# A four-layer convolution and expert-mixing kernel: two differences of the first pair move to GpSimd, and VectorE shares all evictions of the matrix sets from the third to the fourteenth

## The reference

```python
x = x + conv1d(x, w_L0, kernel=9, pad=4, groups=4) + (cond @ cw_L0.T + bias)[:, :, None]
x = x + einsum('boi,bih->boh', sum_k att1[b, k] * W_L1[k], x) + (att1 @ bias_k1)[:, :, None]
x = x + conv1d(x, w_L2, kernel=9, pad=4, groups=4) + (cond @ cw_L2.T + bias)[:, :, None]
x = x + einsum('boi,bih->boh', sum_k att3[b, k] * W_L3[k], x) + (att3 @ bias_k3)[:, :, None]
```

## Time and profile before

| | us |
|---|---|
| median of three runs | 2477.7 |
| lowest, highest | 2477.03, 2478.44 |
| span of the profiled execution, first to last instruction | 2475.0 |
| TensorE busy in the profiled execution | 2456.7 (99%) |
| VectorE busy | 2139.8 (86%) |
| ScalarE busy | 1520.3 (61%) |
| GpSimd busy | 23.4 (1%) |

### The profile page before, as it was taken

The page is one execution under the profiler, slowest core; times in us unless marked ns, Lnnn a source line. Parts: engine busy times, 40 slices in busy tenths (PEclk is TensorE's granted clock), DMA queues, the critical chain, the costliest instruction groups (busy, mean ns, idle before and its releaser), DMA issues.

```text
span 2475.0 us, 99123 instructions
## 1 busy us (share of the span) xinstructions
PE 2456.7 (99%) x45256; PEld 1482.8 (60%) x45256; DVE 2139.8 (86%) x806; ACT 1520.3 (61%) x1120; POOL 23.4 (1%) x28
## 2 busy tenths in 40 slices
PE   8999999999999999999999999999999999999998
PEld 4444444555555555566666666666666666666665
DVE  7988988988988889889889888898898898888984
ACT  6666666666666666666666666666666666665665
POOL 3000000000000000000000000000000000000000
PEclk9999999999999999999999999999999999999999
DMA  9644444444445444444444444444444444444433
GB/s 346 207 131 127 152 144 127 135 152 136 127 138 156 130 127 155 142 127 138 152 135 127 140 155 128 127 157 140 127 140 151 133 127 143 153 127 127 157 108 121
DMA packets 186683, 357.24 MB, mean 144 GB/s; under 512 B 12754, under 2 KB 143834, under 8 KB 154010
## 3 DMA queue, kind: packets, MB, share of 16 engines
q1 hardware_dynamic: 186056, 354.60, 45.7%
q10 hardware_dynamic: 594, 2.13, 0.3%
HBM read 205.69 MB, written 150.99 MB: 144 GB/s over the span
## 4 chain that ended last, share of the span: by engine, by line
PE 97%; DVE 2%; issue 1%; ACT 0%; DVEq 0%; ACTq 0%
PE psum L410 61%; PE psum L481 35%; DVE diff L754 1%; PE psum L379 0%; ACT shared L629 0%; PE psum L353 0%; PE psum L331 0%; ACT diff L629 0%; DVE y L797 0%; DVE y L813 0%; DVE y L838 0%; DVE h L789 0%; ACT y L629 0%; DVE y L816 0%; DVE outb L861 0%
## 5 line engine op out<-in xcount | busy, mean ns | idle before, releaser
L410 PE MATMUL psum<-diff,prod_w 32*64 32x512 f32 x28672 | 1689.2, 588 | 2.9 <-DVE diff L754 0.9
L410 PEld LDWEIGHTS psum<-diff,prod_w 32*64 32x64 f32 x28672 | 963.0, 131 | 624.3 <-issue 295.2
L754 DVE TENSOR_TENSOR diff<-xin 128x2052 f32<-128x2052 f32 x256 | 993.0, 3934 | 286.7 <-PE psum L410 286.7
L481 PE MATMUL psum<-y,mixw 32*64 32x512 f32 x16384 | 1028.9, 588 | 1.9 <-DVE y L816 1.9
L481 PEld LDWEIGHTS psum<-y,mixw 32*64 32x64 f32 x16384 | 581.5, 132 | 338.2 <-issue 179.5
L754 DVE TENSOR_TENSOR diff<-x 128x2055 f32<-128x2055 f32 x255 | 570.4, 2320 | 0.0
L720 ACT ACTIVATE x<-psum,bias_now 128x2048 f32<-128x2048 f32 x128 | 251.7, 1966 | 198.7 <-PE psum L481 198.7
L680 ACT ACTIVATE outb<-psum,bias_now 128x2048 f32<-128x2048 f32 x128 | 251.1, 1962 | 195.3 <-PE psum L481 195.3
L645 ACT COPY shared<-psum 128x2048 f32<-128x2048 f32 x128 | 238.9, 1866 | 171.6 <-PE psum L410 171.6
L838 DVE TENSOR_TENSOR y<-y,shared 128x2048 f32<-128x2048 f32 x126 | 291.2, 2311 | 14.7 <-ACT y L659 14.7
L673 ACT COPY y<-psum 128x2048 f32<-128x2048 f32 x126 | 235.7, 1871 | 91.8 <-PE psum L410 91.8
(11 more groups left out here) (80 smaller groups left out, 106.7 us busy)
## 6 DMA issues: line engine op xcount, KB each, us to landing
xin<-x SPq DMA_DIRECT2D x128, 1024.0 KB, 6.9
out<-outb SPq DMA_DIRECT2D x127, 1024.0 KB, 4.8
mixw<-mix_dram SPq DMA_DIRECT2D x512, 128.0 KB, 5.5
mix_dram<-shared SPq DMA_DIRECT2D x6, 1024.0 KB, 12.7
mix_dram<-y SPq DMA_DIRECT2D x6, 1024.0 KB, 10.4
mix_dram<-diff SPq DMA_DIRECT2D x2, 1024.0 KB, 12.1
mix_dram<-outb SPq DMA_DIRECT2D x2, 1024.0 KB, 14.1
y<-experts ACTq DMA_DIRECT2D x2, 512.0 KB, 4.3
```

The costliest lines, as they stand in the source:

```text
L410: return pe.matmul(psum[cols, half, g, :], prod_w[v][at, kind, s, cols], moving, start=start, stop=stop, skip_group_check=True)
L481: mm = pe.matmul(psum[cols, half, r, :], mixw[home][at, b, g, cols], y[home][at, :, g, b, :], start=g == 0, stop=g == GROUPS - 1)
L754: nc.vector.tensor_tensor(into(kind), in0, in1, op).then_inc(diff_ready[v], 1)
```

## The change

1. GpSimd makes BOTH and SIGNED of pair 0 (`first_diff`), each counted on a new semaphore `first_diffs`. BOTH comes ahead of layer one's tap weights and waits for x of the first pair; SIGNED comes behind them. VectorE makes ONLY_EVEN and ONLY_ODD of pair 0 alone, and each adds two to `diff_ready[0]`, so that later counts stay.
2. `HALVED` now holds 2 to 13. VectorE takes two banks of each of those twelve sets, all ahead of its differences, and waits for the same landed stores as ScalarE from set 10 on.
3. TensorE's first convolution waits for VectorE's halves of sets 12 and 13 too, and for `first_diffs`; its third part waits for `diff_ready[0]` at 4 as before. SyncE waits for `first_diffs` too ahead of x of pair 1.

```diff
-        HALVED = (2, 3, 4, 5, 6)
+        HALVED = tuple(range(2, AHEAD))
...
             load_mix_on(sp, 0, 0)
+            sp.wait_ge(first_diffs, 2)
             sp.wait_ge(diff_ready[0], PRODUCTS)
...
+            def first_diff(kind, op):
+                eighths = xin[:].rearrange("p (m c) -> p c m", c=BLOCK)
+                pool.tensor_tensor(diff_of(0, kind).rearrange("p (s c) -> p s c", s=PH)[:, :, 0:T - 1],
+                                   eighths[:, 0:PH, 1:T], eighths[:, PH:, 0:T - 1], op).then_inc(first_diffs, 1)
+
             for v in range(2):
...
+                if v == 0:
+                    pool.wait_ge(x_loaded, 16 * PB)
+                    pool.wait_ge(edges_clear, 1)
+                    first_diff(BOTH, ALU.add)
                 pool.wait_ge(taps_loaded[v], 16 * 3)
...
                 pool.tensor_tensor(w[:, SIGNED], middle, w[:, SIGNED], ALU.subtract).then_inc(taps_ready, 1)
+                if v == 0:
+                    first_diff(SIGNED, ALU.subtract)
...
-                pe.wait_ge(diff_ready[v], diffs[0])
+                pe.wait_ge(diff_ready[v] if made is None else made, diffs[0])
...
-                pe.wait_ge(diff_ready[v], diffs[1])
+                pe.wait_ge(diff_ready[v] if made is None else made, diffs[1])
                 pe.wait_ge(sem_b, count_b)
+                if made is not None:
+                    pe.wait_ge(*upper_taken(AHEAD - 1))
...
-                    conv(0, 0, taken(AHEAD - 2), taken(AHEAD - 1), (1, 2, 4), nothing)
+                    pe.wait_ge(*upper_taken(AHEAD - 2))
+                    conv(0, 0, taken(AHEAD - 2), taken(AHEAD - 1), (1, 2, PRODUCTS), nothing, made=first_diffs)
...
             for j in HALVED:
                 dve.wait_ge(agg_pe, j + 1)
+                if j >= 10:
+                    dve.wait_ge(agg_stored[same_home_before(j)], 16)
                 nc.vector.tensor_copy(homes[home_of[j]][:, PH // 2:PH], psum[:, half_of(j), PH // 2:PH, :]
                                       ).then_inc(agg_taken["dve"], 1)
             dve.wait_ge(edges_clear, 1)
-            diff_of_xin(0, (BOTH, SIGNED, ONLY_EVEN, ONLY_ODD))
+            diff_of_xin(0, (ONLY_EVEN, ONLY_ODD))
```

More of the change, by code:

```diff
@@ L133, in conditioned_layers @@
         x_loaded = sem("x_loaded")
+        first_diffs = sem("first_diffs")
         diff_ready = [sem(f"diff_ready{v}") for v in range(2)]
@@ L424, in divided_set, with conv @@
                 return mm
-            def conv(v, n, a_free, b_free, diffs, late, halves=(A, B_HALF), second=nothing, odd=None):
+            def conv(v, n, a_free, b_free, diffs, late, halves=(A, B_HALF), second=nothing, odd=None, made=None):
                 A, B_HALF = halves
@@ L737, in diff_of_xin @@
                 at = [eighths[:, PH * (q % 2):PH * (q % 2 + 1), q // 2:q // 2 + T - 1] for q in range(4)]
-                make_diffs(0, at, kinds, lambda kind: diff_of(0, kind).rearrange(
+                make_diffs(0, n, at, kinds, lambda kind: diff_of(0, kind).rearrange(
                     "p (s c) -> p s c", s=PH)[:, :, 0:T - 1])
@@ L747, in diff_of_x2, with make_diffs @@
                 at = [x2[:, start:start + size] for start in (HALF - 1, 0, HALF, 1)]
-                make_diffs(1, at, kinds, lambda kind: diff_of(1, kind)[:, 0:size])
-            def make_diffs(v, at, kinds, into):
+                make_diffs(1, n, at, kinds, lambda kind: diff_of(1, kind)[:, 0:size])
+            def make_diffs(v, n, at, kinds, into):
                 for kind in kinds:
@@ L753, in make_diffs @@
                                     SIGNED: (at[2], at[1], ALU.subtract), ONLY_ODD: (at[3], at[1], ALU.subtract)}[kind]
-                    nc.vector.tensor_tensor(into(kind), in0, in1, op).then_inc(diff_ready[v], 1)
+                    nc.vector.tensor_tensor(into(kind), in0, in1, op).then_inc(diff_ready[v], PRODUCTS // len(kinds)
+                                                                               if whole(n) and (v, n) == (0, 0) else 1)
             nc.vector.memset(hid[0]["att_t"][:], 0.0).then_inc(blank, 1)
```

## The result

The changed kernel takes 2482.82 us (median of 13 runs, 2481.99 to 2484.23) against 2477.59 us before (13 runs, 2476.84 to 2479.47): 5.2 us slower, a ratio of 1.0021 with a 95% interval of 1.0013 to 1.0028. The profiled execution of the changed kernel has a span of 2482.1 us and took 2483.88 us. So 1.8 us lie around that span, and 1.8 to 1.9 in every run on record, not 2.7.

A forecast was written before the change was run, and what follows sets the result against it. TensorE holds 96% of the chain, and the start of the first convolution's third part sets the end. Its 6.75 us delay plus 0.25 for the clock made 7.0, so 2484.7 us; range 2478.8 to 2487.5, forecast's own 2482.6 to 2485.9.

The forecast's parts named there:

- What bounds: Start of the kernel: any shift of the first convolution's third part moves VectorE's first output and the end equally.
- T3: Start of the first convolution's third part, which needs ONLY_EVEN: 43.9 before, forecast 50.65, 6.75 us later.
- the restart: TensorE going on after waiting for VectorE's difference, at 95.86 before; forecast at 102 to 103.
- Evictions: VectorE's copy of set 13 waits for set 5's store, so VectorE is free for differences at 37.45, not 26.32.
- D: Time of one GpSimd difference of pair 0 with stepped operands: forecast 7.7 us, from 4.6 in a row times 1.7.
- Blocking: Two-operand VectorE and GpSimd instructions run one after the other, so ONLY_EVEN waits for SIGNED and runs 42.9 to 46.75.
- Rival 2: VectorE and GpSimd don't block each other in long instructions: third part about 46.3, +2.4 us, 2480.1; chance 0.09.
- rival 1: GpSimd reads steps at little extra cost, 4.6 to 6.8 us a difference: not over 0.2% slower, 2479.0; chance 0.25.
- Small things: GpSimd's later weights, VectorE's outputs, x of pair 1 and stores behind it: weights and outputs still meet twice, cost 0.
- The clock: TensorE's waits may lower its clock when the third part starts: 0.25 us added, the middle of 0 to 0.5.
- the last step of the sum: Whole kernel: the 7.0 us shift of the profiled span, 2475.0 to 2482.0, put on the median, 2477.7 to 2484.7.
- The reading of L323: GpSimd's one-operand operation L323 ran beside VectorE's L810, neither longer than alone; held to change nothing in the sum.

The follow-up runs named there:

- rearranged: Kernel before, with GpSimd making weights then BOTH alone, VectorE halving sets 2 to 8 and 12, SIGNED ahead of 12, ONLY_ODD awaited where read: 2476.47 us, ratio 0.9995.
- two more sets: Kernel before, with VectorE also halving sets 7 and 8 and TensorE awaiting ONLY_ODD only where it reads it: 2476.55 us, ratio 0.9996.
- differences alone: Changed kernel with evictions shared only for sets 2 to 6, as before, so only GpSimd's two differences are new: 2483.88 us, ratio 1.0026 to the kernel before.
- without VectorE on set 13: Changed kernel, but ScalarE takes set 13 whole: 2482.43 us, one run.
- changed, again: The changed kernel once more, unaltered: 2482.61 us, ratio 1.0020 to the kernel before.
- weights first: Changed kernel with GpSimd's weights ahead of both its differences: 2478.69 us, ratio 1.0005 to the kernel before.

## Why the prediction was right, point by point

- **What bounds.** T3, VectorE's first output and the restart moved by 6.7, 6.5 and 6.6 us, and every experiment in which the third part waits moved the restart with it (51.8 to 52.5 us between them). Right for those. It does not hold where the third part came sooner: I count 120 records to 42.1 in *rearranged* and to 42.8 in *two more sets*, 1.8 and 1.1 us sooner, and the restart came 0.9 sooner and 0.4 later, because GpSimd's second weights did not move along.
- **Evictions.** Free at 37.45 was forecast, 37.79 measured, with the wait of 1.35 us ahead of set 13's copy. Right; without GpSimd's differences they cost 8.7 us.
- **D.** 7.7 was forecast from VectorE's factor, 7.70 and 7.61 measured. The lower bound of 4.6 for elements in a row was 4.54. The half as much again of the Trainium skill ("GPSIMD Engine Reference", section 7, Performance pitfalls for Q7 kernels) made an estimate of 6.9; the trace has 7.70 over 4.54, a factor of 1.7. For one operand no run has so many elements in a row; scaled from 1.49 us for 512 as the two-operand operation scales (4.54 over 1.26), that would be 5.4 us, an estimate, and the step's factor 1.4.
- **Blocking.** ONLY_EVEN from 42.9 to 46.75 was forecast, its end measured at 46.74. Rival 2 falls here and in three experiments (*differences alone*, *without VectorE on set 13*, *changed, again*); rival 1 fell with D, and *weights first* shows the same work without blocking at 5 us less in the third part.
- **Small things.** GpSimd's second weights met VectorE's outputs twice (2.29 and 2.28), as forecast.
- **The clock.** The 0.25 us were not spent in the profiled run: after 3.86 us without a matmul the granted clock was low while TensorE worked on SIGNED (64 records in 5.07 us where I had put 3.6; mean 0.59 from 43.0 to 46.5), and it was full again from 50.6 to 54.0. That loss was hidden in the wait for VectorE's differences, which lasted 2.50 us instead of the 4 I forecast. What it can cost when it falls there, 0.6 us, was forecast as up to 0.5.
- **The size.** Mis-sized was the last step of the sum: the shift of 7.0 us was put on the median, where 5.2 was measured. Its closeness to the 7.1 us between the two spans is in part luck: the mechanism gave 6.6 at the restart, the 0.25 for the clock was not spent, and 0.5 came from behind the restart, for which the sum had no term. I took 2.7 us as lying around the span, but 1.8 do, so the profiled execution before was some 0.9 us faster than its median; the changed one was 1.1 us slower than its own. The landing of x, which the third part of the changed kernel follows one for one, is a possible source of the second, and it isn't shown. So 2482.82 came out just inside the forecast's own range, 2482.6 to 2485.9.
- **The reading of L323.** I took it from one row that a one-operand GpSimd operation leaves VectorE alone. Over stepped operands it halved VectorE's speed. Why L810 showed nothing beside L323, and 1.53 beside the same kind of operation in the rearranged kernel, stays open.

## What to carry to other kernels

An engine with 1% load is not a free place for work whose instructions hold up those of the engine it is to relieve: count the instructions of both that read two SBUF operands and see whether they can meet in time. Where they met here, their durations added: moving the weights ahead of the differences on GpSimd took away 4 of the 5 us. And work put ahead in an in-order queue costs that queue what its last item waits for (here a store's landing), not only its own time.

## What the runs showed of the hardware that I had not expected

A GpSimd operation with one stepped operand took 7.3 us for 2052 elements, nearly the 7.7 of one with two. Beside it a VectorE `tensor_tensor` went at about half speed (1.7 us lost in 3.55, 2.3 in 4.2) and GpSimd lost nothing, while two-operand operations on both sides ran one behind the other, down to one of 0.22 us that took 3.94. Operands in a row don't fit either picture fully: beside a one-operand operation VectorE lost 0, 0.3 and 0.4 us in different places, and one such GpSimd operation that came second took 2.34 us instead of 1.49.
